# A graph network on one Trainium2 core: drains behind the gathers of GpSimd, and two loaded numbers range-checked

## The chip, the core and the metric

The kernel runs on one core of a Trainium2 chip. It is written by hand: each engine (TensorE or PE, VectorE or DVE, ScalarE or ACT, GpSimd or POOL, SyncE or SP) has its own instruction stream, and the streams meet in semaphores. The metric is the device time of one execution in microseconds (us), as the median of several runs.

## What is computed

6250 nodes with 128 features, 206,250 edges (100,000 random pairs in both directions, and a loop at each node). Three graph convolutions follow each other, then one attention layer with two heads. Cut to what matters:

```python
# three times, on the result of the one before
norm = deg_inv_sqrt[row] * deg_inv_sqrt[col] * edge_weight
xw = einsum('ni,tio->tno', x, W)                     # four edge types
out = segment_sum(xw[edge_type, col] * norm[:, None], row) + b
z = leaky_relu(out, 0.01)
# x = layernorm(x + (x + z1 + z2 + z3) / 4), then the attention
alpha = leaky_relu(a_src[src] + a_dst[dst], 0.2)      # softmax over the edges of a node
out = segment_sum(alpha[:, :, None] * xp[src], dst) + bias
# x = layernorm(x + out)
```

In each layer every edge fetches one row of 128 numbers from a table in HBM and adds it, scaled, to its node.

## The kernel before

**Preparation.** The edges are sorted by node on the chip, and the lists of rows to fetch and of slots are made (`rec_idx`, `gcn_at`, `gat_at`, `gat_need`).

**Layers.** A tile is 128 edges. A layer has 1612 tiles, in 52 turns of 31. For each tile GpSimd issues one indirect DMA (L737, a gather) that fetches 128 rows of 512 bytes into a ring `g_rows` of 93 tiles. `FOURS` cuts a turn into eight groups, seven of four tiles and one of three; the tiles of group u count their landing on semaphore `s_g[u]`. When GpSimd has issued a group it waits until the group before has landed and posts that on `s_land` (`pass_landed`, L711 to L714). Four times in a turn (`SUBS`) it waits, from turn 3 on, for `s_copied`, so that it doesn't overwrite a slot of the ring still to be read (`wait_apart`, L145 to L147: a wait and an increment of a semaphore nobody needs).

ScalarE takes four tiles in a step, 465 steps a layer. It loads their four ring slots and the number of the last tile from `gcn_at` (`slots_of`, L896), waits for `s_gpe` and for `s_land`, and scales the four tiles into `g_step` (L912). TensorE sums them into the nodes by a one-hot matrix `g_hot` that VectorE makes (L1196, L1620), and VectorE adds the sum to `acc` (L1634). In the last 13 or so steps of a layer the table of the next one is made batch by batch (`next_z`, `products`, `rows_of`) and written to HBM; GpSimd starts the next layer when it is there.

**Attention.** 403 groups of four tiles, 451 steps. GpSimd gathers a group into one of eight slots of `a_roll` (L762); from the ninth group on it first loads from `gat_need` which step must be over (L758, range-checked) and waits for it (`sa["cand"]`). Behind its four gathers it waits until the group before has landed and adds one to `s_land`. SyncE goes through the steps: it loads a group number for `e_dst` (L534, range-checked), then group and slot (L540, two numbers in one load, not checked), waits for `s_land`, and copies the slot to `a_rows` (L549). ScalarE, TensorE and VectorE then do the softmax and the sums.

Nothing but these streams sets the order; there is no scheduler.

Of the kernel before, what the change touches and what calls it, by code (L numbers as in the profile page):

```python
# [77 lines left out]
CH = 4  # L78
CCOLS = COLS // CH
# [3 lines left out]
RING = RING_TURNS * TURN  # L83
# [3 lines left out]
GP = 4  # L87
# [6 lines left out]
ROLL = 8  # L94
GAT_GROUPS = EDGES_PAD // (GAT.tiles * P)
AHEAD = BW - 2
SUBS = [(0, 7), (8, 15), (16, 23), (24, TURN - 1)]
FOURS = [range(t, min(t + 4, TURN)) for t in range(0, TURN, 4)]
# [69 lines left out]
def gnn_kernel(nc, x, src, dst, etype, weight, w1, b1, w2, b2, w3, b3, w_gat, att_src, att_dst,  # L168
               bias_gat, out):
    ctx = ExitStack()  # L170
    with ctx:
# [70 lines left out]
        most = sb("most", [BW, 1], F32, sort)  # L242
# [209 lines left out]
        def _(sp):  # L452
# [79 lines left out]
            def body(q):  # L532
                if q.live(2):
                    group = sp.value_load(gat_at[0:1, bass.ds(q.at(2), 1), 0], min_val=0, max_val=GAT_GROUPS - 1)  # L534
                    if q.live(2 - R):
                        wait_apart(sp, sa["cand"], q.at(2 - R, 1, 1), s_apart)
                    sp.dma_start(e_dst[:, q.slot(2), :].unsqueeze(1), dst_groups[:, bass.ds(group, 1), :]
                                 ).then_inc(s_el[q.slot(2)], 16)
                if q.live(0):
                    _, (tile, slot) = nc.values_load_multi_w_load_instructions(  # L540
                        gat_at[0:1, bass.ds(q.at(0), 1), :].rearrange("p g k -> p (g k)"),
                        engines=(mybir.EngineType.SP,), min_val=0, max_val=GAT_GROUPS - 1,
                        skip_runtime_bounds_check_because="a step less the begun blocks, at most the last group")
                    slot = nc.s_assert_within(slot, 0, ROLL - 1,
                                              skip_runtime_bounds_check_because="a group modulo the ring")
                    if q.live(-R):
                        wait_apart(sp, sa["msg"], q.at(-R, 1, 1), s_apart)
                    wait_apart(sp, s_land, tile + (3 * CH * CCOLS + 1), s_apart)
                    sp.dma_start(a_rows[:, q.slot(0), :, :].rearrange("p t k -> p (t k)").unsqueeze(1),  # L549
                                 a_roll[:, bass.ds(slot, 1), :, :].rearrange("p g t k -> p g (t k)")  # L550
                                 ).then_inc(s_ag[q.slot(0)], 16)
# [13 lines left out]
        def _(pool):  # L565
# [150 lines left out]
            for layer in range(3):  # L716
                for k in range(4):
                    pool.wait_ge(s_tw[k], 16 * (layer + 1) * len(range(k, NB, 4)))
                if layer:
                    pool.wait_ge(s_copied, layer * GRP.steps)  # L720
                for q in range(SORT.steps):
                    c, u = divmod(q, CSPANS)
                    if q == 0 and not layer:
                        pool.wait_ge(s_idx0, 1)
                    if (q == 1 or c and u == 0) and not layer:
                        pool.wait_ge(s_idx, c + 1)
                    for low, high in SUBS:
                        steps = CSTEPS * c + u * TURN + high + 1 - RING + AHEAD
                        if u < RING_TURNS:
                            last = u * TURN + high - RING == -1  # L730
                            steps = CSTEPS * c if last else steps - CSTEPS + CCOLS
                        if q >= RING_TURNS:
                            wait_apart(pool, s_copied, layer * GRP.steps - (-steps // GP), s_apart)
                        for t in range(low, high + 1):
                            tile = TURN * q + t
                            at = rec_idx[:, tile:tile + 1] if q else first_idx[:, t:t + 1]
                            pool.indirect_dma_start(  # L737
                                out=g_rows[:, tile % RING, :], out_offset=None, in_=gcn_tables[layer % 2],
                                in_offset=bass.IndirectOffsetOnAxis(ap=at, axis=0),
                            ).then_inc(s_g[t // 4], 16)  # L740
                            n = q * len(FOURS) + t // 4
                            if t == FOURS[t // 4][-1] and n:
                                pass_landed(layer, n - 1)
                pass_landed(layer, SORT.steps * len(FOURS) - 1)
# [11 lines left out]
            for g in range(GAT_GROUPS):  # L756
                if g >= ROLL:
                    need = pool.value_load(gat_need[0:1, g - ROLL:g - ROLL + 1], min_val=1, max_val=GAT.steps)  # L758
                    wait_apart(pool, sa["cand"], need, s_apart)
                for t in range(T):  # L760
                    n = g * T + t
                    pool.indirect_dma_start(  # L762
                        out=a_roll[:, g % ROLL, t, :], out_offset=None, in_=gat_table,
                        in_offset=bass.IndirectOffsetOnAxis(ap=src_plane[:, n:n + 1].bitcast(U32), axis=0),
                    ).then_inc(s_g[g % ROLL], 16)
                if g:
                    wait_apart(pool, s_g[(g - 1) % ROLL], rolled(g - 1), s_land)
            wait_apart(pool, s_g[(GAT_GROUPS - 1) % ROLL], rolled(GAT_GROUPS - 1), s_land)
# [4 lines left out]
        def _(act):  # L773
# [86 lines left out]
            def scale_rows(layer):  # L860
# [32 lines left out]
                        last.then_inc(s_added, 1)  # L893

                def slots_of(q):
                    _, values = nc.values_load_multi_w_load_instructions(  # L896
                        gcn_at[32:33, bass.ds(q.at(0), 1), :].rearrange("p g k -> p (g k)"),
                        engines=(mybir.EngineType.Activation,), min_val=0, max_val=CH * CCOLS - 1,
                        skip_runtime_bounds_check_because="a step less the begun blocks, at most the last tile")
                    return values  # L900

                def scale(q, values):
                    j = q.slot(0) % 3
                    *found, tile = values
                    slots = [nc.s_assert_within(v, 0, RING - 1,
                                                skip_runtime_bounds_check_because="a tile modulo the ring")
                             for v in found]
                    if q.live(-3) or layer:
                        act.wait_ge(s_gpe, q.at(-3, 1, GRP.steps * layer + 1))
                    act.wait_ge(s_land, tile + (CH * CCOLS * layer + 1))  # L910
                    for k in range(GP):
                        last = nc.scalar.activation(g_step[:, j, k, :].unsqueeze(1),  # L912
                                                    g_rows[:, bass.ds(slots[k], 1), :],
                                                    ACT.Copy, scale=rec_w[:, bass.ds(q.at(0, GP, k), 1)])
                    last.then_inc(s_copied, 1)
# [963 lines left out]
```

## Time and profile before

| | us |
|---|---|
| median of 3 runs without a profile | 8958.33 (8957.9 to 8960.3) |
| span of the profiled execution | 11925.3 |
| first gather of the layers starts | 691.5 |
| first gather of the attention starts | 8505.5 |
| last gather starts | 11826.8 |
| GpSimd busy | 6395.8 |

The profiled execution is a third longer than the runs without a profile. Durations of single instructions are taken from it, and waits only where they can be shown to stand in the other runs as well. In the rows, POOL is GpSimd's engine and POOLq its sequencer, which reads the stream, waits for semaphores, loads registers and hands instructions to the engine. "idle before" is time of the engine, and what follows the arrow is who ended it; "issue" means that nothing in the profile did.

### The profile page before, as it was taken

What the parts mean: (1) busy time and instruction counts of PE and PEld (TensorE: products, weight loads), DVE (VectorE), ACT (ScalarE), POOL (GpSimd) and SP (SyncE); (2) the same over time, 40 slices, a digit from 0 to 9 for tenths busy, and PEclk for the clock granted to TensorE, in tenths of its full rate; (3) what the DMA queues carried; (4) which work ended last, traced back from release to release, by engine and by line L of the source; (5) the groups of instructions that cost most, each with busy time, mean ns of one, the idle gap of its engine ahead of it and who ended that gap; (6) DMA issues with size and microseconds to landing.
All of it is one profiled execution on the core that took longest, in us unless ns stands there. A gap on an engine that the chain in (4) does not pass through costs nothing.

```text
span 11925.3 us, 149378 instructions
## 1 busy us (share of the span) xinstructions
PE 5307.0 (45%) x32765; PEld 4105.0 (34%) x32766; DVE 4574.2 (38%) x12940; ACT 3992.0 (33%) x12236; POOL 6395.8 (54%) x6521
## 2 busy tenths in 40 slices
PE   5843434434533434343433434343444444444444
PEld 4632322223322323232322323232344444444444
DVE  9952222222322212222322222222555555555556
ACT  6522222222322222222322222222455454445455
POOL 1656566565456565656466565656344444444443
PEclk9975655656655655565655556555566666666666
DMA  1011111111221111111211111111122222222222
GB/s 47 35 42 43 41 44 43 41 44 41 65 55 44 40 44 40 44 40 44 76 42 44 40 44 40 44 40 44 49 69 70 68 71 69 69 68 69 70 69 65
DMA packets 432687, 612.42 MB, mean 51 GB/s; under 512 B 232038, under 2 KB 249491, under 8 KB 432539
## 3 DMA queue, kind: packets, MB, share of 16 engines
q0 software_dynamic: 208832, 428.96, 13.7%
q1 hardware_dynamic: 223707, 182.02, 4.6%
q14 instruction: 121, 0.99, 0.0%
q8 instruction: 27, 0.44, 0.0%
HBM read 437.29 MB, written 51.28 MB: 41 GB/s over the span
## 4 chain that ended last, share of the span: by engine, by line
another core or an unknown queue 48%; DVE 16%; issue 15%; PE 8%; ACTq 5%; DVEq 4%; ACT 3%; POOL 0%; DMA 0%; POOLq 0%; SPq 0%
DVEq L1604 3%; PE bank L1196 3%; ACT g_step L912 3%; ACTq L896 2%; DVE a_miss L1717 2%; PE wide L1196 2%; DVE g_hot L1620 2%; ACTq L912 1%; DVE acc L1634 1%; DVE a_max L1722 1%; DVE lo_hot L1262 1%; DVE acc L1788 1%; PE bank L1191 1%; DVE v_hot L1387 1%
## 5 line engine op out<-in xcount | busy, mean ns | idle before, releaser
L737 POOL DMA_INDIRECT g_rows<-gcn_table,rec_idx x4743 | 4487.1, 946 | 2894.2 <-ACT g_step L912 1484.6
L912 ACT ACTIVATE g_step<-g_rows,rec_w 128x128 f32 x5580 | 1791.5, 390 | 5679.7 <-remote 4618.4
L762 POOL DMA_INDIRECT a_roll<-gat_table,src_plane x1612 | 1524.6, 946 | 1801.0 <-ACT a_cand L937 1375.4
L1634 DVE TENSOR_TENSOR acc<-acc,bank 128x512 f32 x930 | 637.9, 686 | 3828.8 <-remote 3238.9
L1191 PE MATMUL bank<-zeros 1*128 1x512 bf16 x930 | 490.9, 528 | 2909.9 <-DVE acc L1634 2104.6
L1196 PE MATMUL bank<-g_step,g_hot 128*128 128x128 f32 x7440 | 1621.7, 386 | 128.4 <-issue 50.6
L1196 PEld LDWEIGHTS bank<-g_step,g_hot 128*128 128x128 f32 x7440 | 1391.8, 280 | 487.9 <-issue 487.9
L1222 PE MATMUL bank<-a_msg,a_hot 128*128 128x130 f32 x3608 | 798.9, 389 | 1648.7 <-DVE a_msg L1768 1635.0
L1222 PEld LDWEIGHTS bank<-a_msg,a_hot 128*128 128x128 f32 x3608 | 685.6, 283 | 1786.3 <-DVE a_msg L1768 1452.3
L1191 PEld LDWEIGHTS bank<-zeros 1*128 1x128 bf16 x930 | 89.9, 97 | 3099.0 <-DVE acc L1634 2163.3
L937 ACT ACTIVATE a_cand<-a_miss,a_rows 128x128 f32<-128x128 bf16 x3608 | 1095.9, 386 | 14.9 <-DMA a_rows<-a_roll 8.8
L1634 DVE TENSOR_TENSOR acc<-acc,wide 128x512 f32 x465 | 318.2, 684 | 1879.5 <-remote 1618.0
L1620 DVE TENSOR_TENSOR g_hot<-bank,rec_lo 128x512 f32<-128x512 f32 x1395 | 952.0, 683 | 1.8 <-DVE mv L1677 0.2
L1191 PE MATMUL wide<-zeros 1*128 1x512 bf16 x465 | 244.0, 525 | 1429.6 <-DVE acc L1634 1141.6
L1196 PE MATMUL wide<-g_step,g_hot 128*128 128x128 f32 x3720 | 803.5, 383 | 42.3 <-issue 19.3
L930 ACT ACTIVATE a_hot<-a_miss 128x512 f32<-128x512 bf16 x451 | 284.0, 630 | 1558.0 <-DVE a_miss L1717 1428.6
L1196 PEld LDWEIGHTS wide<-g_step,g_hot 128*128 128x128 f32 x3720 | 690.1, 278 | 220.7 <-issue 220.7
L1213 PE MATMUL wide<-ident,a_cand 128*128 128x128 f32 x3608 | 696.5, 357 | 99.1 <-ACT a_cand L937 83.2
L1213 PEld LDWEIGHTS wide<-ident,a_cand 128*128 128x128 f32 x3608 | 563.9, 186 | 114.5 <-ACT a_cand L937 78.2
L1722 DVE TENSOR_REDUCE a_max<-wide 128x2 f32<-128x1024 f32 x451 | 550.0, 1220 | 107.6 <-remote 69.4
L1741 DVE TENSOR_TENSOR a_z<-bank,a_rows 128x8 f32<-128x8 f32 x451 | 74.0, 164 | 1305.9 <-remote 1302.7
L1191 PEld LDWEIGHTS wide<-zeros 1*128 1x128 bf16 x465 | 44.9, 96 | 1525.1 <-DVE acc L1634 1173.7
(272 smaller groups left out, 5880.3 us busy)
## 6 DMA issues: line engine op xcount, KB each, us to landing
a_rows<-a_roll SPq DMA_DIRECT2D x451, 264.0 KB
g_rows<-gcn_table,rec_idx POOLq DMA_INDIRECT x4743
gcn_table<-rows SPq DMA_DIRECT2D x147, 256.0 KB
a_roll<-gat_table,src_plane POOLq DMA_INDIRECT x1612
e_dst<-by_dst_dst SPq DMA_DIRECT2D x451, 2.0 KB
gat_table<-acc SPq DMA_DIRECT2D x7, 462.0 KB
out_x<-xs SPq DMA_DIRECT2D x6, 448.0 KB
gcn_slots<-nothing SPq DMA_DIRECT2D x4, 468.0 KB, 6.8
```

The lines of the kernel that those rows point to most:

```text
L737: pool.indirect_dma_start(out=g_rows[:, tile % RING, :], out_offset=None, in_=gcn_tables[layer % 2], in_offset=bass.IndirectOffsetOnAxis(a ...
L762: pool.indirect_dma_start(out=a_roll[:, g % ROLL, t, :], out_offset=None, in_=gat_table, in_offset=bass.IndirectOffsetOnAxis(ap=src_plane[ ...
L912: last = nc.scalar.activation(g_step[:, j, k, :].unsqueeze(1), g_rows[:, bass.ds(slots[k], 1), :], ACT.Copy, scale=rec_w[:, bass.ds(q.at(0 ...
L937: last = nc.scalar.activation(a_cand[:, w, h, t, :], a_miss[:, j, t, :], ACT.Identity, scale=-BIG, bias=a_rows[:, j, t, ROW - HEADS + h:RO ...
L1191: nc.tensor.matmul(sums_of(j)[:, :], zeros[0:1, 0:1].to_broadcast([1, P]), zeros[0:1, 0:1].to_broadcast([1, GP * D]), start=True, stop=False)
L1196: last = nc.tensor.matmul(sums_of(j)[:, bass.ds(places[k], D)], g_hot[:, j % 3, k, :], g_step[:, j % 3, k, :], start=False, stop=(k == GP ...
L1213: last = nc.tensor.transpose(wide[:, w, h, t, :], a_cand[:, w, h, t, :], ident[:, :])
L1222: last = nc.tensor.matmul(pv_ps(j), a_hot[:, j, t, :], a_msg[:, j, t, :], start=(t == 0), stop=(t == T - 1))
L1604: _, values = nc.values_load_multi_w_load_instructions(ap, engines=(mybir.EngineType.DVE,), min_val=0, max_val=NB - 1, skip_runtime_bounds ...
L1620: V.tensor_tensor(g_hot[:, j, :, :], spread(iota_ps.unsqueeze(1), [P, GP, P]), spread(lo.unsqueeze(2), [P, GP, P]), ALU.is_equal).then_inc ...
L1634: V.tensor_tensor(dst_ap, dst_ap, sums_of(j).rearrange("p (k d) -> p k d", k=GP), ALU.add).then_inc(s_gadd, 1)
L1722: V.tensor_reduce(a_max[:, m, :], wide[:, m % 2, :, :, :].rearrange("p h t e -> p h (t e)"), AX.X, ALU.max).then_inc(sa["max"], 1)
```

## The change

`pool.drain()` is put behind the last gather of each group: behind the fourth (or third) in a layer, ahead of the wait in `pass_landed`, and behind the fourth in the attention. That is 8 x 52 x 3 = 1248 drains in the layers and 403 in the attention. A drain holds GpSimd's sequencer until its engine is idle.

Two numbers are checked against their range when they are loaded: the last tile's number that ScalarE waits with in a layer's step, and SyncE's group number in an attention step. For that the one load of several numbers is split in two, and the slot in SyncE's load is checked as well.

```diff
@@ SyncE, a step of the attention
-                    _, (tile, slot) = nc.values_load_multi_w_load_instructions(
-                        gat_at[0:1, bass.ds(q.at(0), 1), :].rearrange("p g k -> p (g k)"),
-                        engines=(mybir.EngineType.SP,), min_val=0, max_val=GAT_GROUPS - 1,
...
+                    tile = sp.value_load(gat_at[0:1, bass.ds(q.at(0), 1), 0], min_val=0, max_val=GAT_GROUPS - 1)
+                    slot = sp.value_load(gat_at[0:1, bass.ds(q.at(0), 1), 1], min_val=0, max_val=ROLL - 1)
@@ GpSimd, the layers
                             ).then_inc(s_g[t // 4], 16)
+                            if t == FOURS[t // 4][-1]:
+                                pool.drain()
                             n = q * len(FOURS) + t // 4
                             if t == FOURS[t // 4][-1] and n:
                                 pass_landed(layer, n - 1)
@@ GpSimd, the attention
                     ).then_inc(s_g[g % ROLL], 16)
+                    if t == T - 1:
+                        pool.drain()
                 if g:
                     wait_apart(pool, s_g[(g - 1) % ROLL], rolled(g - 1), s_land)
@@ ScalarE, a step of a layer
                 def slots_of(q):
+                    tile = act.value_load(gcn_at[32:33, bass.ds(q.at(0), 1), GP], min_val=0,
+                                          max_val=CH * CCOLS - 1)
                     _, values = nc.values_load_multi_w_load_instructions(
-                        gcn_at[32:33, bass.ds(q.at(0), 1), :].rearrange("p g k -> p (g k)"),
-                        engines=(mybir.EngineType.Activation,), min_val=0, max_val=CH * CCOLS - 1,
...
+                        gcn_at[32:33, bass.ds(q.at(0), 1), 0:GP].rearrange("p g k -> p (g k)"),
+                        engines=(mybir.EngineType.Activation,), min_val=0, max_val=RING - 1,
...
-                    return values
+                    return *values, tile
```

On ScalarE a layer's step starts with these instructions before (TENSOR_LOAD is a load into registers, REGISTER_ALU and ISA are register arithmetic, and ACTIVATE scales one tile):

```order
L896 TENSOR_LOAD gcn_at
L910 REGISTER_ALU
L912 ISA
L912 ACTIVATE g_step<-g_rows,rec_w 128x128
L912 ISA
```

and with these now:

```order
L896 TENSOR_LOAD gcn_at
L896 ISA x2
L898 TENSOR_LOAD gcn_at
L909 REGISTER_ALU
L911 ISA
L911 ACTIVATE g_step<-g_rows,rec_w 128x128
```

A second load, register arithmetic and a check stand ahead of the first ACTIVATE. On SyncE an attention step, from the second copy of `e_dst` on, is before:

```order
L537 DMA e_dst<-by_dst_dst 128x4
L540 TENSOR_LOAD gat_at
L146 REGISTER_ALU
L549 ISA
L549 DMA a_rows<-a_roll 128x528
```

and now:

```order
L537 DMA e_dst<-by_dst_dst 128x4
L540 TENSOR_LOAD gat_at
L540 ISA x2
L541 TENSOR_LOAD gat_at
L541 ISA x2
L146 REGISTER_ALU
L545 ISA
L545 DMA a_rows<-a_roll 128x528
```

One load has become two with a check behind each, ahead of the copy to `a_rows`. GpSimd's gathers keep their order; the drains stand between them and are not listed in such a view.

## Rows read from the trace of the kernel before

**Rows 1.** Page, part 1: busy us (share of span) x instructions by engine

```profile
PE 5307.0 (45%) x32765; PEld 4105.0 (34%) x32766; DVE 4574.2 (38%) x12940; ACT 3992.0 (33%) x12236; POOL 6395.8 (54%) x6521
```

**Rows 2.** Waits of GpSimd: who <- for whom: us in total, times, longest

```profile
POOL g_rows L737 <- ACT g_step L912: 1484.6, 191, 43.8
POOL a_roll L762 <- ACT a_cand L937: 1375.4, 312, 11.6
```

**Rows 3.** Groups by line on GpSimd: xcount | busy us, mean ns | idle before

```profile
L737 POOL DMA_INDIRECT g_rows<-gcn_table,rec_idx x4743 | 4487.1, 946 | 2894.2 <-ACT g_step L912 1484.6 <-issue 1246.4 <-DMA g_rows<-gcn_table,rec_idx 162.8
L762 POOL DMA_INDIRECT a_roll<-gat_table,src_plane x1612 | 1524.6, 946 | 1801.0 <-ACT a_cand L937 1375.4 <-issue 410.2 <-DMA a_roll<-gat_table,src_plane 11.9
...
L737 POOL DMA_INDIRECT g_rows<-gcn_table,first_idx x93 | 90.3, 971 | 225.0 <-DMA gcn_table<-rows 185.6 <-issue 24.7 <-DVE first_idx L1506 12.0
...
L748 POOL MEMSET acc<- 128x14 f32 x7 | 0.9, 124 | 125.1 <-ACT acc L858 125.1
```

**Rows 4.** Timeline of GpSimd, three stretches: start us, us, what, [idle before <-releaser]

```profile
691.47 1.00 POOL L737 DMA_INDIRECT g_rows<-gcn_table,first_idx  x1 [11.97 <-DVE first_idx L1506]
...
2121.42 0.95 POOL L737 DMA_INDIRECT g_rows<-gcn_table,rec_idx  x1 [0.30 <-DMA g_rows<-gcn_table,rec_idx]
...
2128.93 0.94 POOL L737 DMA_INDIRECT g_rows<-gcn_table,rec_idx  x1 [0.30 <-issue]
...
11826.75 0.95 POOL L762 DMA_INDIRECT a_roll<-gat_table,src_plane  x1 [0.30 <-issue]
```

**Rows 5.** Timeline of ScalarE in a layer, a step that waits for nobody

```profile
2113.31 1.28 ACT L912 ACTIVATE g_step<-g_rows,rec_w 128x128 f32 x4 [0.63 <-issue]
```

**Rows 6.** Timeline of VectorE in the attention, the same line in two steps

```profile
9004.72 0.17 DVE L1741 TENSOR_TENSOR a_z<-bank,a_rows 128x8 f32<-128x8 f32 x1 [7.43 <-remote]
...
9008.89 0.17 DVE L1741 TENSOR_TENSOR a_z<-bank,a_rows 128x8 f32<-128x8 f32 x1
```

**Rows 7.** Timeline of GpSimd around waits, in a layer and in the attention

```profile
1621.09 0.94 POOL L737 DMA_INDIRECT g_rows<-gcn_table,rec_idx  x1 [6.22 <-ACT g_step L912]
...
8660.60 0.94 POOL L762 DMA_INDIRECT a_roll<-gat_table,src_plane  x1 [6.21 <-ACT a_cand L937]
...
8666.85 0.95 POOL L762 DMA_INDIRECT a_roll<-gat_table,src_plane  x1 [0.31 <-issue]
```

**Rows 8.** Line 147 on GpSimd's sequencer, three single instructions: duration ns, first to last start

```profile
L147 POOLq EVENT_SEMAPHORE  x1: 17/17/17, 1620.3 to 1620.3; - x1
...
L147 POOLq EVENT_SEMAPHORE  x1: 17/17/17, 8659.8 to 8659.8; - x1
...
L147 POOLq EVENT_SEMAPHORE  x1: 17/17/17, 8666.9 to 8666.9; - x1
```

**Rows 9.** Line 758 between 8666 and 8668 us: duration ns, first to last start

```profile
L758 POOLq TENSOR_LOAD <-gat_need x1: 293/293/293, 8667.0 to 8667.0; - x1
...
L758 POOLq SEQ_ASSERT  x1: 18/18/18, 8667.5 to 8667.5; - x1
```

**Rows 10.** Timeline of GpSimd at the start of the program

```profile
0.39 0.12 POOL L1868 MEMSET const-uint8-127<- 128x1 uint8 x1
0.91 0.24 POOL L566 IOTA iota<- 128x128 f32 x1 [0.40 <-POOLq L1868]
```

**Rows 11.** Line 1868 on GpSimd's sequencer: xcount: duration ns, first to last start

```profile
L1868 POOLq EVENT_SEMAPHORE  x2: 17/17/17, 0.6 to 0.7; - x2
...
L1868 POOLq DRAIN  x1: 189/189/189, 0.4 to 0.4; - x1
```

**Rows 12.** Stretches: PE, PEld, DVE, ACT, POOL busy us (x), PEclk, DMA share, GB/s

```profile
1659.50:1660.00 0.50, 0.00 (x0) 0.00 (x0) 0.00 (x0) 0.00 (x0) 0.05 (x1) 0.50 0.00 0
1660.00:1660.50 0.50, 0.00 (x0) 0.00 (x0) 0.00 (x0) 0.00 (x0) 0.00 (x0) 0.50 0.43 123
```

**Rows 13.** Timeline of TensorE and of ScalarE in a layer, one step

```profile
1606.52 2.07 PE L1196 MATMUL bank<-g_step,g_hot 128*128 128x128 f32 x8 [0.26 <-issue]
...
1619.03 1.28 ACT L912 ACTIVATE g_step<-g_rows,rec_w 128x128 f32 x4 [12.75 <-remote]
```

More of the change, by code:

```diff
@@ L539, in body @@
                 if q.live(0):
-                    _, (tile, slot) = nc.values_load_multi_w_load_instructions(
-                        gat_at[0:1, bass.ds(q.at(0), 1), :].rearrange("p g k -> p (g k)"),
-                        engines=(mybir.EngineType.SP,), min_val=0, max_val=GAT_GROUPS - 1,
-                        skip_runtime_bounds_check_because="a step less the begun blocks, at most the last group")
-                    slot = nc.s_assert_within(slot, 0, ROLL - 1,
-                                              skip_runtime_bounds_check_because="a group modulo the ring")
+                    tile = sp.value_load(gat_at[0:1, bass.ds(q.at(0), 1), 0], min_val=0, max_val=GAT_GROUPS - 1)
+                    slot = sp.value_load(gat_at[0:1, bass.ds(q.at(0), 1), 1], min_val=0, max_val=ROLL - 1)
                     if q.live(-R):
@@ L895, in slots_of @@
                 def slots_of(q):
+                    tile = act.value_load(gcn_at[32:33, bass.ds(q.at(0), 1), GP], min_val=0,
+                                          max_val=CH * CCOLS - 1)
                     _, values = nc.values_load_multi_w_load_instructions(
-                        gcn_at[32:33, bass.ds(q.at(0), 1), :].rearrange("p g k -> p (g k)"),
-                        engines=(mybir.EngineType.Activation,), min_val=0, max_val=CH * CCOLS - 1,
-                        skip_runtime_bounds_check_because="a step less the begun blocks, at most the last tile")
-                    return values
+                        gcn_at[32:33, bass.ds(q.at(0), 1), 0:GP].rearrange("p g k -> p (g k)"),
+                        engines=(mybir.EngineType.Activation,), min_val=0, max_val=RING - 1,
+                        skip_runtime_bounds_check_because="a tile modulo the ring")
+                    return *values, tile
                 def scale(q, values):
                     j = q.slot(0) % 3
[L904 to L907, printed above, removed]
+                    *slots, tile = values
                     if q.live(-3) or layer:
```

## The prediction

> **What bounds the kernel now.** I read the page's head and engine totals first [rows 1]. GpSimd (POOL) is busy 54% of the span, more than any other engine, and no engine is near full. The waits of POOL come next [rows 2]: 1484.6 us (191 times) for ScalarE's copies in the layers and 1375.4 us (312 times) for ScalarE in the attention. The profiled execution took 11925 us, the median without a profile is 8958, so it must first be settled which of these waits exist in the timed runs.
>
> Count GpSimd's work. There are 4743 + 93 gathers in the three layers and 1612 in the attention, 6448 in all, 946 ns each [rows 3]. In a stretch without waits one starts every 1.25 us (2121.42 to 2128.93 is 6 intervals of 1.252), with 0.30 us "issue" between them [rows 4]. 6448 x 1.252 = 8073 us. Around them stand parts with no gather: 691 us until the first, two layer changes of 93 us (185.6), 125 us ahead of the attention and 98 us behind the last gather [rows 3, 4]: 1100 us. Together 9173 us. The same from the other side: the profiled span without the waits for ScalarE, 11925 - 1485 - 1375 + 503 x 0.30 (the normal gap that each of these 503 waits contains) = 9216. The median of 8958 is below both. So in a timed run GpSimd issues gathers without a pause from the first to the last, the waits for ScalarE belong to the profiled execution, and the missing 215 us are a preparation or a pitch a little shorter than under the profile (1.22 us would do). The other engines have room beside it: where ScalarE isn't waiting, a layer step of four tiles takes it 1.28 + 0.63 = 1.91 us [rows 5] against GpSimd's 5.0; a VectorE step of the attention takes 4.17 us [rows 6], 451 x 4.17 = 1881 us against GpSimd's 1612 x 1.25 = 2018.
>
> **The drains.** A drain stops GpSimd's sequencer until the engine is idle; only then does it read the landing semaphore, post s_land and send the next gather. Now it works ahead. At 8666.9 it posts the landing of one group [rows 8] while the second gather of the next group is just starting [rows 7]; that group's two last gathers are already queued, and the load of the following number (0.29 us), its range check [rows 9] and the wait for ScalarE all vanish behind them: the gaps stay 0.30. A drain gives up exactly this overlap. There are 8 in each of 52 turns of 3 layers, 1248, and 403 in the attention, 1651 in all.
>
> Price of one in a layer. The trace has two cases in which GpSimd's queue was empty: in the layers the waiting instruction runs at 1620.3 and the gather starts at 1621.09; in the attention 8659.8 and 8660.60 [rows 7, 8]. I take 0.75 us and 0.77 us from wait to start. The one DRAIN of GpSimd in the trace starts at 0.37 (0.4 in its row), lasts 189 ns, and ends 0.05 us behind the last MEMSET's end (0.39 + 0.12); the next semaphore instruction is at 0.6 [rows 10, 11]: about 0.1 us from idle to the first wait. So 0.1 + 0.75 = 0.85 us stand between two gathers where 0.30 do now: +0.55. 1248 x 0.55 = 686 us. In front of every second group of turns 3 to 51 stands a second wait, for s_copied, at about 0.1 us (the step from the wait at 8666.9 to the load at 8667.0 [rows 8, 9]): 588 x 0.1 = 59 us.
>
> Price of one in the attention. Behind the drain come the landing wait, then the load at +0.1 us, the range check until +0.6 (8666.9 to 8667.5 [rows 8, 9]), the wait for ScalarE at about +0.65 and 0.77 to the start: 0.1 + 0.65 + 0.77 = 1.5 against 0.30, +1.2. 395 groups have the load: 474 us; the first eight 0.55 each: 4.
>
> None of this lies beside other work, since GpSimd is the bound. Drains: 686 + 59 + 478 = 1223 us.
>
> The bounds of this price. Below: the engine's shortest restart from an empty queue is the IOTA that starts at 0.91 behind the semaphore instruction at 0.7 [rows 10, 11], 0.2 us; 0.1 + 0.2 is the gap that is there now, so a gather that restarts as fast as an IOTA costs nothing. I stay with the gathers' own rows. Above: the 0.30 us between two gathers may be work of the engine behind the recorded end. Then the drain ends up to 0.30 later: + 1651 x 0.30 = 495, in all 1718 us. The Trainium skill (Perfetto Trace Analysis, DMA Instruction — SWDGE) says for this engine that the recorded end is the last descriptor written and that the instruction finishes after it; by that page the price lies between my value and this upper end.
>
> **What is queued behind a drain.** On GpSimd: the post of s_land for the group before (now at the second gather of a group, then behind its fourth, 2.5 us later) and all later gathers. Who waits for the post is ScalarE in the layers, SyncE in the attention. GpSimd may run at least 45 tiles or 8 groups ahead, some 50 us, so the late post delays only the ends of stages, by 2.5 us each; I leave it out.
>
> **The range checks.** GpSimd's own load with its check takes 0.5 us of its sequencer (8667.0 to 8667.5 [rows 9]); I take 0.6 us for one on SyncE or ScalarE too, where a load may first have to wait for the instructions before it. SyncE gets a second load and two checks in each of 451 attention steps, about 0.8 us, 361 us if it were bare. It lies beside GpSimd's 6.2 us per group: nothing. ScalarE gets a second load and a check in each of 1395 steps: a step goes from 1.91 to 2.5 us, beside GpSimd's 5.0 or more for the same four tiles: hidden, except where no gather is left. There, at a layer's end, ScalarE still has about 28 steps (some 15 of catching up, then the last 13 among the next layer's rows): 28 x 0.6 = 17 us a layer, 50 in all; part of it lies beside VectorE's and TensorE's work, so I take 35 out of 0 to 50. If GpSimd were not the bound, all 1395 would be bare: 837 us.
>
> **The sum.** 8958 + 1223 + 35 = 10216 us. The durations are of the profiled execution; the base is the median, since the profile's own excess (2967 us) is waits that the drains would partly fill there.
>
> **The rivals.**
> Slower, as forecast (queue lost at each drain): 10216, between 9700 and 10850. For it: every number above is this engine's own. Against: the restart was seen only behind waits, never behind a drain.
> Cheap drain: the sequencer's work on the next gather is mostly hidden and only 0.1 to 0.2 us is lost per drain, 165 to 330 us: 9120 to 9320 with the rest. The IOTA's short restart [rows 10, 11] speaks for it; that 403 of these gathers sit behind a load and a check speaks against.
> Drain waits for the data: after a gather that ended at 1659.55, packets still move at 1660.0 to 1660.5 [rows 12], so a drain that lasts until they have landed takes 1.0 us more: + 1651 = 11870. The one DRAIN in the trace [rows 11] had no DMA behind it and can't tell.
> No loss, or a gain: if GpSimd waits for ScalarE in the timed runs too, a drain only fills such a wait. The trace shows how: ScalarE's step at 1619.03 starts after 12.75 us of waiting, 10 us after TensorE's last matmul of the step before has ended (1606.52 + 2.07) [rows 13], in one of GpSimd's pauses (6.22 us ahead of 1621.09 [rows 7]). If gathers hold other engines' releases back, pauses let them through sooner. It decides once these waits exceed 1223 us in a timed run, and gives 8958 or less, say 8850. The count above leaves no room for them.
> The drain does nothing (the engine is idle when it comes): 8958 + 35. The steady 0.30 us gap [rows 4] with a queue behind it speaks against.
>
> **How the numbers follow.** Queue lost 0.73; cheap 0.11; waits for data 0.07; filled waits or a gain 0.04; nothing 0.03; the rest, some other stall, 0.02. The likeliest gives 10215. The range runs from 9250 (half of the cheap case) to 10850 (the upper end of the price with the range checks' 50 and some more), which leaves about 0.17 outside. A measurement of this kernel can tell about 0.2% from no change. Faster by more: 0.03 (a gain). Within: 0.03. Slower: 0.94.
>
> **What the changed profile would show.** Three gaps of 0.30 us between gathers and every fourth 0.85 in the layers, 1.5 in the attention; DRAIN of 2 to 3 us each on GpSimd, since it is reached while gathers are queued; s_land's post behind the fourth gather. Wrong would be: every fourth gap still near 0.30 or 0.45 (cheap), or near 1.9 and 2.5 (waits for data); other engines' busy times unchanged in all cases. If the gaps are as said and the time moved by less than half of 1223, the claim that GpSimd bounds the timed runs falls.

## The result, and the profile after

| | before | after |
|---|---|---|
| median without a profile | 8958.15 us | 13031.51 us |
| lowest to highest, 4 runs each | 8957.9 to 8960.3 | 13030.99 to 13036.31 |
| span of the profiled execution | 11925.3 | 13034.2 |

The change makes the kernel slower by 45%: the ratio is 1.4548, with a 95% interval of 1.4527 to 1.4569. That is 4073 us for 1651 drains, 2.47 us each. The forecast was 10215 us, 1257 us more than before. Its direction was right and the measured cost was 3.2 times the forecast one.

Read this profile with one caution. The profiled execution of before took a third longer than its other runs, that of after took the time of its other runs. A comparison of the two profiles would show 1109 us, not 4073. So the profile of the first experiment, in which the drains alone are missing (span 8945.1, as long as its other runs), is what after has to be compared with.

The engines of after (page, part 1: busy us, share of the span, instructions), which answer to [rows 1], and the shares of the chain that ended last:

```profile
PE 5925.3 (45%) x32765; PEld 4641.6 (36%) x32766; DVE 4687.3 (36%) x12940; ACT 3955.9 (30%) x12236; POOL 6397.1 (49%) x6521
...
issue 44%; POOL 34%; POOLq 15%; DVE 3%; PE 2%; ACT 1%; DMA 1%; ACTq 0%; DVEq 0%; SPq 0%
```

GpSimd is busy as long as before, 6397 us against 6396. None of its work takes longer; the time lies between its instructions. Half of the chain is GpSimd (POOL and its sequencer POOLq), and most of the rest is "issue", idle time that nothing in the profile explains. The 15% of POOLq are mostly the records of the drains where they lie beside a gather that is still running. Behind the last gather of a group a drain leaves no busy time of the engine and no semaphore event, so there the profile shows its cost as "issue".

GpSimd's groups of after by line (busy us, mean ns, idle time ahead and who ended it), which answer to [rows 3]:

```profile
L733 POOL DMA_INDIRECT g_rows<-gcn_table,rec_idx x4743 | 4491.3, 947 | 4285.3 <-issue 4269.4 <-ACT g_step L911 15.9
L760 POOL DMA_INDIRECT a_roll<-gat_table,src_plane x1612 | 1524.6, 946 | 1693.2 <-issue 1571.4 <-ACT a_cand L936 118.1 <-DMA gat_table<-acc 3.7
...
L733 POOL DMA_INDIRECT g_rows<-gcn_table,first_idx x93 | 91.4, 983 | 157.8 <-issue 84.3 <-DMA gcn_table<-rows 62.6 <-DVE first_idx L1505 10.8
```

A gather still takes 947 ns. Ahead of the layers' gathers GpSimd sits idle for 4285 us and hardly any of it is a wait for ScalarE. The timeline of GpSimd in a layer and in the attention (start us, us, what, idle before) shows where:

```profile
3001.52 0.95 POOL L733 DMA_INDIRECT g_rows<-gcn_table,rec_idx  x1 [2.66 <-issue]
...
3005.28 0.95 POOL L733 DMA_INDIRECT g_rows<-gcn_table,rec_idx  x1 [0.30 <-issue]
3008.75 0.95 POOL L733 DMA_INDIRECT g_rows<-gcn_table,rec_idx  x1 [2.52 <-issue]
...
11009.41 0.95 POOL L760 DMA_INDIRECT a_roll<-gat_table,src_plane  x1 [3.30 <-issue]
```

Three gaps of 0.30 us are as before [rows 4]; every fourth is 2.5 to 2.7 us in this stretch of a layer and 3.30 in the attention. Of the two in the lines, the longer one (2.66) has the second wait, for `s_copied`, in it. The prediction had 0.85 and 1.5 for these.

What happens in the gap of 2.52 us is seen from three answers of the trace: the drain of this group on GpSimd's sequencer (xcount: duration ns min/median/max, first and last start), the pieces of the chain in order of time (L710 is the first instruction that has a record behind the drain, it posts `s_land`), and the stretches of half a microsecond (engines' busy us, PEclk, DMA share, GB/s).

```profile
L738 POOLq DRAIN  x1: 5287/5287/5287, 3002.7 to 3002.7; - x1
```

```profile
3006.22 1.77 issue
3007.99 0.02 POOLq L710
3008.01 0.74 issue
```

```profile
3006.00:3006.50 0.50, 0.00 (x0) 0.00 (x0) 0.00 (x0) 0.00 (x0) 0.22 (x1) 0.50 0.01 0
3006.50:3007.00 0.50, 0.00 (x0) 0.00 (x0) 0.00 (x0) 0.00 (x0) 0.00 (x0) 0.50 0.17 57
3007.00:3007.50 0.50, 0.00 (x0) 0.00 (x0) 0.00 (x0) 0.00 (x0) 0.00 (x0) 0.50 0.25 74
3007.50:3008.00 0.50, 0.00 (x0) 0.00 (x0) 0.00 (x0) 0.00 (x0) 0.00 (x0) 0.50 0.00 0
```

The sequencer reaches the drain at 3002.7, with the second gather of the group just starting. The fourth gather ends on the engine at 3006.22. The drain holds for another 1.77 us, until 3007.99, and in this time the rows of that gather arrive: the DMA share is 0.01, then 0.17 and 0.25, then 0. Then 0.76 us pass until the next gather starts, the restart that the prediction took from [rows 7, 8]. So a gap of 2.52 is 1.77 of drain and 0.75 of restart.

Everyone else waits for GpSimd. The first entry of the waits of after (who, for whom: us, times, longest):

```profile
ACT g_step L911 <- POOLq L710: 6860.5, 1204, 20.3
```

ScalarE waits 1204 times for the post of line 710. In the profile of before it was GpSimd that waited for ScalarE [rows 2]. That isn't the work of the drains: in the profile of experiment 1, without a drain, ScalarE already waits 1096 times for this post, 3784 us in all.

### The profile page after: what moved, and what is told of

Read it like the earlier page. It is cut to its first block, busy times and chain, and to the rows that moved or that the text cites. A ratio compares the mean times of both kernels' runs of the same rounds, so it can differ in the third digit from the quotient of the medians.

```text
span 13034.2 us, 159230 instructions
## 1 busy us (share of the span) xinstructions
PE 5925.3 (45%) x32765; PEld 4641.6 (36%) x32766; DVE 4687.3 (36%) x12940; ACT 3955.9 (30%) x12236; POOL 6397.1 (49%) x6521
## 4 chain that ended last, share of the span: by engine, by line
issue 44%; POOL 34%; POOLq 15%; DVE 3%; PE 2%; ACT 1%; DMA 1%; ACTq 0%; DVEq 0%; SPq 0%
POOL g_rows L733 26%; POOLq L738 10%; POOL a_roll L760 8%; POOLq L765 3%; POOLq L756 1%; ACT a_cand L936 1%; DVE lo_hot L1261 1%; DVE v_hot L1386 1%; PE wide L1081 0%; DMA a_rows<-a_roll 0%; DVE p_hot L1261 0%; DVE hi_hot L1261 0%; PE wide L1159 0%; PE wide L1095 0%; POOLq L147 0%
## 5 line engine op out<-in xcount | busy, mean ns | idle before, releaser
L733 POOL DMA_INDIRECT g_rows<-gcn_table,rec_idx x4743 | 4491.3, 947 | 4285.3 <-issue 4269.4
L1195 PE MATMUL bank<-g_step,g_hot 128*128 128x128 f32 x7440 | 1884.3, 433 | 3399.5 <-ACT g_step L911 3391.8
L1195 PEld LDWEIGHTS bank<-g_step,g_hot 128*128 128x128 f32 x7440 | 1620.5, 321 | 3845.6 <-issue 3845.6
L760 POOL DMA_INDIRECT a_roll<-gat_table,src_plane x1612 | 1524.6, 946 | 1693.2 <-issue 1571.4
L1195 PE MATMUL wide<-g_step,g_hot 128*128 128x128 f32 x3720 | 946.2, 435 | 1798.5 <-ACT g_step L911 1798.5
L1195 PEld LDWEIGHTS wide<-g_step,g_hot 128*128 128x128 f32 x3720 | 814.1, 323 | 2021.6 <-issue 2021.6
L1212 PE MATMUL wide<-ident,a_cand 128*128 128x128 f32 x3608 | 821.9, 403 | 1497.1 <-ACT a_cand L936 1497.0
L1212 PEld LDWEIGHTS wide<-ident,a_cand 128*128 128x128 f32 x3608 | 656.4, 210 | 1532.7 <-ACT a_cand L936 1278.4
L1221 PEld LDWEIGHTS bank<-a_msg,a_hot 128*128 128x128 f32 x3608 | 753.3, 307 | 94.5 <-DVE a_msg L1767 73.6
L1767 DVE SCALAR_TENSOR_TENSOR a_msg<-bank,a_rows 128x520 f32<-128x520 f32 x451 | 315.1, 699 | 1031.2 <-ACT bank L948 1031.2
L591 POOL DMA_INDIRECT gcn_slots<-run,at_u x52 | 285.5, 5491 | 390.8 <-issue 380.8
L1716 DVE TENSOR_TENSOR a_miss<-bank,a_lo 128x256 bf16<-128x256 f32 x902 | 375.0, 416 | 0.1
```

The costliest lines, as they stand in the source:

```text
L733: pool.indirect_dma_start(out=g_rows[:, tile % RING, :], out_offset=None, in_=gcn_tables[layer % 2], in_offset=bass.IndirectOffsetOnAxis(a ...
L760: pool.indirect_dma_start(out=a_roll[:, g % ROLL, t, :], out_offset=None, in_=gat_table, in_offset=bass.IndirectOffsetOnAxis(ap=src_plane[ ...
L1195: last = nc.tensor.matmul(sums_of(j)[:, bass.ds(places[k], D)], g_hot[:, j % 3, k, :], g_step[:, j % 3, k, :], start=False, stop=(k == GP ...
L1212: last = nc.tensor.transpose(wide[:, w, h, t, :], a_cand[:, w, h, t, :], ident[:, :])
L1221: last = nc.tensor.matmul(pv_ps(j), a_hot[:, j, t, :], a_msg[:, j, t, :], start=(t == 0), stop=(t == T - 1))
```

## The experiments

Two theories were compared at the start. **Landing**: a drain of GpSimd holds until all that GpSimd has asked of the DMA engines has landed. **Engine idle**, the prediction's own: it holds until the engine has done its work, and something else (a fixed toll of the drain, or the late post of `s_land`) makes the rest. All kernels of the network start from the kernel after, with both range checks in, so the drains alone without these checks weren't tried.

**1. The range checks alone.**

```diff
-                            if t == FOURS[t // 4][-1]:
-                                pool.drain()
...
-                    if t == T - 1:
-                        pool.drain()
```

> The changed kernel without any drain: the two range checks alone. Theory (all of the loss is in the drains): 8958 us, at most 35 more at the layers' ends. Rival (the split loads on ScalarE or SyncE reach the path): 9300 or more, up to 837 us more if ScalarE's steps were bare. The profiled execution should again be near 11900, if its excess over the timed runs belongs to a stream of gathers without drains.

Measured: 8949.75 us (10 runs, 8946.94 to 8951.04) beside 8948.27 of before, ratio 1.0001 (0.9991 to 1.0011). The checks cost nothing that the runs can tell. They are there: the number of ScalarE's first loads and of the range checks behind them (SEQ_ASSERT), with the duration of one (ns), and then GpSimd's waits in this trace, are

```profile
L892 ACTq TENSOR_LOAD <-gcn_at x1395: 268/273/974, 745.8 to 6834.1; - x200
L892 ACTq SEQ_ASSERT  x1395: 18/18/29, 746.5 to 6834.6; - x200
```

```profile
POOL g_rows L733 <- issue: 1371.9, 4503, 0.3
POOL a_roll L758 <- issue: 478.8, 1571, 0.3
...
POOL a_roll L758 <- ACT a_cand L932: 5.2, 17, 0.3
```

This profile is the picture of the kernel without drains that the prediction had to infer. GpSimd waits 4503 and 1571 times, never longer than 0.3 us: a gather follows a gather from end to end, and the long waits for ScalarE of [rows 2] aren't there. The expectation that this profile would again be near 11900 us did not come true: its span is 8945.1. The idle time by group gives the account of the change:

```profile
L733 POOL DMA_INDIRECT g_rows<-gcn_table,rec_idx x4743 | 4490.1, 947 | 1445.0 <-issue 1346.0 <-DMA g_rows<-gcn_table,rec_idx 96.6 <-ACT g_step L907 2.4
L758 POOL DMA_INDIRECT a_roll<-gat_table,src_plane x1612 | 1522.8, 945 | 494.5 <-issue 478.8 <-DMA a_roll<-gat_table,src_plane 7.0 <-ACT a_cand L932 5.2
...
L733 POOL DMA_INDIRECT g_rows<-gcn_table,first_idx x93 | 90.2, 969 | 94.7 <-DMA gcn_table<-rows 55.3 <-issue 25.9 <-DVE first_idx L1501 11.9
```

With drains the idle time ahead of these three groups is longer by 2840 (4285.3 - 1445.0), 1199 (1693.2 - 494.5) and 63 us (157.8 - 94.7), 4102 in all. The spans differ by 4089 (13034.2 - 8945.1). So the whole loss is idle time of GpSimd ahead of a gather; the other engines and the ends of stages add nothing that shows.

**2 and 3. The drains of one part alone.** Kernel 2 leaves out the second of the two removed pieces above (the drain in the attention), kernel 3 the first (the drains in the layers).

> Drains in the three layers alone (1248). Theory landing (a drain lasts until the gathers' data has landed, gaps of 2.53 to 2.65 us as in the changed kernel's trace, 2.3 more than the normal 0.30): 8958 + 1248 x 2.3 = 11830 us. Theory of the forecast (only the queue is lost, 0.55 each): 9700. If the losses of layers and attention do not add up (this plus the one with attention drains alone is not 8958 + 4073), they share a limit.

> Drains in the attention alone (403). Theory landing (gaps of 3.28 us, 2.97 more): 8958 + 403 x 2.97 = 10155 us. Theory of the forecast (1.2 each): 9440. If the sum with the layers' kernel falls short of 4073, part of the loss is shared.

Measured: the layers' 1248 drains alone give 11827.87 us, ratio 1.3218 (1.3196 to 1.3240), +2880 beside 8948.27. The attention's 403 alone give 10149.3, ratio 1.1342 (1.1323 to 1.1361), +1201. The two add up to 4081 against 4073 for both, so the two parts share no limit. One costs 2.31 us in a layer and 2.98 in the attention, which is the gaps of the timeline less the 0.30 that was there. The difference of 0.67 fits what stands behind the drain in the attention, the load and check of `gat_need`; the prediction had 0.65 for it (1.2 - 0.55), or 0.59 between its averages, in which the waits for `s_copied` are spread over the layers' drains (478 / 403 - 745 / 1248).

**4. Every second drain.**

```diff
-                            if t == FOURS[t // 4][-1]:
+                            if t == FOURS[t // 4][-1] and t // 4 % 2:
...
-                    if t == T - 1:
+                    if t == T - 1 and g % 2:
```

> Drains behind every second group alone (624 in the layers, each ahead of two waits, and 201 in the attention). Theory landing, each drain for itself: 624 x 2.35 + 201 x 2.97 = 2063, so 11020 us. Rival (what costs is that gathers get behind once and for all, or a fixed toll of draining at all): clearly not half of 4073.

Measured: 11135.31 us, ratio 1.2442 (1.2421 to 1.2463), +2187, which is 150 more than half of 4073, and 124 more than expected. GpSimd's timeline behind such a drain shows a longer gap, 2.88 us instead of 2.66 or 2.52:

```profile
3011.99 0.94 POOL L733 DMA_INDIRECT g_rows<-gcn_table,rec_idx  x1 [2.88 <-issue]
```

So a drain isn't independent of what lies before it: with eight gathers since the last drain instead of four, one costs about 0.2 us more. This was not expected by either theory and led to experiments 9 and 10.

**5. No drain, but a wait for the group's own landing.** GpSimd waits for the landing semaphore of the group that it has just issued, not of the one before.

```diff
-                            if t == FOURS[t // 4][-1]:
-                                pool.drain()
                             n = q * len(FOURS) + t // 4
-                            if t == FOURS[t // 4][-1] and n:
-                                pass_landed(layer, n - 1)
-                pass_landed(layer, SORT.steps * len(FOURS) - 1)
+                            if t == FOURS[t // 4][-1]:
+                                pass_landed(layer, n)
...
-                    if t == T - 1:
-                        pool.drain()
-                if g:
-                    wait_apart(pool, s_g[(g - 1) % ROLL], rolled(g - 1), s_land)
-            wait_apart(pool, s_g[(GAT_GROUPS - 1) % ROLL], rolled(GAT_GROUPS - 1), s_land)
+                wait_apart(pool, s_g[g % ROLL], rolled(g), s_land)
```

> No drain; GpSimd waits behind each group for the landing of that same group instead of the one before. Theory landing (the drain is in effect this wait): the gap is the landing 1.57 us after the gather's end, about 0.05 to see it, and the restart 0.75 (attention: load, check and 0.77), so 2.07 to 2.17 more than 0.30 in the layers and 2.73 in the attention: 8958 + 2640 + 1100 = 12700 us. Rival (a drain costs by itself, whatever has landed): the landing lies beside other work, and this kernel stays below 11500.

Measured: 12772.62 us, ratio 1.4260 (1.4236 to 1.4284), beside 8957.31: 94% of what the drains cost (3815 of 4073 us), without one drain. Its timeline:

```profile
3001.18 0.94 POOL L733 DMA_INDIRECT g_rows<-gcn_table,rec_idx  x1 [2.31 <-DMA g_rows<-gcn_table,rec_idx]
```

Here the profile names the releaser, the DMA of the gather. From the gather's end to its landing it is 2.31 - 0.75 of restart, about 1.56 us. The chain of this trace gives it directly (start us, us; the DMA piece counts from the start of the gather, which keeps the engine for 0.94 us):

```profile
2997.93 2.47 DMA g_rows<-gcn_table,rec_idx
...
3000.43 0.02 POOLq L710
```

2.47 - 0.94 is 1.53 us to the landing, and 0.02 later comes the post. A drain's 1.77 is this landing and 0.2 us more. Here `s_land` is posted for the group itself and as soon as it has landed, and still 94% of the cost is there; so the late post of `s_land` isn't what costs.

**6. The wait of 5 and a drain behind it.** When the drain comes, everything has landed.

```diff
                             if t == FOURS[t // 4][-1]:
                                 pass_landed(layer, n)
+                                pool.drain()
...
                 wait_apart(pool, s_g[g % ROLL], rolled(g), s_land)
+                pool.drain()
```

> As the kernel that waits for its own group, and then a drain, when nothing of GpSimd's is under way. Theory landing: a drain with all landed costs 0.05 to 0.2 us: 80 to 330 us more than without, about 12900. Rival (a drain behind DMAs takes a fixed 1.7 us from the engine's end on, or from its own start on): 1651 x 1.7 = 2800 more, about 15500.

Measured: 13315.66 us, ratio 1.4867 (1.4842 to 1.4891), +543 over kernel 5 or 0.33 us a drain, more than the 80 to 330 us that were expected. A second landing or a fixed toll of 1.7 us a drain would have given 15500. The drain's own record has shrunk from 5.3 us, in which the rest of the group and the landing lay, to

```profile
L740 POOLq DRAIN  x1248: 282/364/4649, 700.1 to 9920.5; - x179
```

So it is mainly the landing that the drain of the kernel after waits for. But 364 ns with nothing left to wait for is twice the 189 ns of [rows 11].

**7. Engine idle, made by hand.** No drain; a MEMSET of one column behind each group, and a wait for its semaphore. The engine has then finished its gathers; their data may be on the way.

```diff
+            def engine_idle():
+                idles[0] += 1
+                nc.gpsimd.memset(idle[:, :], 0.0).then_inc(s_idle, 1)
+                pool.wait_ge(s_idle, idles[0])
...
-                                pool.drain()
+                                engine_idle()
...
-                        pool.drain()
+                        engine_idle()
```

> No drain; behind each group a memset of one column on GpSimd and a wait for its semaphore: this waits until the engine has done its gathers, but not for their data. It is what the forecast took a drain for. By the forecast's prices (queue lost: memset about 0.1, 0.1 to see it, restart 0.75 or in the attention 1.4, less 0.30): 0.65 in a layer, 1.3 in the attention: 8958 + 811 + 524 = 10290 us, between 9900 and 10700. Theory landing says the same, and that the difference to the changed kernel is the wait for the data. Rival (the memset itself waits for the data): near 13000.

Measured: 10412.39 us, ratio 1.1623 (1.1604 to 1.1643). This is the event that the prediction priced, and it lies 2% above the forecast of 10215, inside its range. The gaps in a layer and in the attention:

```profile
3005.96 0.94 POOL L742 DMA_INDIRECT g_rows<-gcn_table,rec_idx  x1 [0.30 <-issue]
3006.90 0.12 POOL L711 MEMSET idle<- 128x1 f32 x1
3007.93 0.95 POOL L742 DMA_INDIRECT g_rows<-gcn_table,rec_idx  x1 [0.91 <-POOL idle L711]
```

```profile
9006.10 0.12 POOL L711 MEMSET idle<- 128x1 f32 x1
9007.69 0.95 POOL L769 DMA_INDIRECT a_roll<-gat_table,src_plane  x1 [1.47 <-issue]
```

From gather to gather 1.03 us in this place of a layer (0.12 + 0.91) and 1.59 in the attention, of which 0.12 is the MEMSET. Without the MEMSETs themselves (1651 x 0.12 = 198 us) the 1455 us of this kernel are 1257. The MEMSET also starts right at the gather's end: the 0.30 us between two gathers is not work of the engine that the MEMSET has to wait for. The upper end of the prediction's price (0.30 more per drain) had stood on that.

**8. GpSimd alone, the drain behind different things.** One small kernel without the network: 12 times each a gather of 128 rows of 128 bytes, of 512 bytes and of 5120 bytes with a drain behind it, four gathers of 512 bytes and a drain, a gather, its landing and a drain, a plain DMA and a drain, a MEMSET and a drain, and this again while SyncE's own DMA of 3 MB is under way.

```python
for r in range(12):
    gather(one[:, r, :], x, s_b)
    pool.drain()
...
for r in range(12):
    gather(landed[:, r, :], x, s_e)
    pool.wait_ge(s_e, 16 * (r + 1))
    pool.drain()
```

> Not the network: GpSimd alone, 12 times each a gather of 128 rows of 128, 512 and 5120 bytes and a drain; four gathers of 512 bytes and a drain; a gather, a wait for its landing and a drain; a plain DMA of GpSimd and a drain; a memset and a drain; and the same while SyncE's load of 3.1 MB is under way. Theory landing: the drain ends 0.2 us after the last landing, so its end moves with the size of the row (1.7 us after the gather's end at 512 bytes, clearly more at 5120), it is short behind the wait (0.2 us) and behind the memsets, SyncE's load or not. Rival (fixed): 1.7 us after the gather's end at all sizes, and also behind the wait. Rival (the drain waits for every DMA of the core): some 10 us behind the first memset under SyncE's load.

Measured: the drains, in the order just given (128, 512, 5120 bytes, four gathers, landed, plain DMA, MEMSET, MEMSET beside SyncE's DMA), by duration:

```profile
L59 POOLq DRAIN  x12: 2471/2526/2790, 13.6 to 47.2; - x12
...
L63 POOLq DRAIN  x12: 2796/2852/2941, 50.2 to 87.2; - x12
...
L67 POOLq DRAIN  x12: 4647/5074/5179, 90.6 to 151.8; - x12
...
L72 POOLq DRAIN  x12: 5332/5356/5388, 158.8 to 239.0; - x12
...
L77 POOLq DRAIN  x12: 113/113/126, 247.7 to 285.4; - x12
...
L80 POOLq DRAIN  x12: 2087/2148/2361, 286.0 to 315.3; - x12
...
L84 POOLq DRAIN  x12: 157/158/177, 317.5 to 320.2; - x12
...
L89 POOLq DRAIN  x12: 152/157/166, 321.4 to 323.8; - x12
```

The timeline for the three row sizes, and the times from issue to landing (part 6, last number, us):

```profile
17.14 0.97 POOL L53 DMA_INDIRECT small<-in_x,idx  x1 [2.14 <-issue]
...
53.89 0.95 POOL L53 DMA_INDIRECT one<-in_x,idx  x1 [2.48 <-issue]
...
96.34 0.94 POOL L53 DMA_INDIRECT large<-in_x,idx  x1 [4.62 <-issue]
```

```profile
direct<-in_x POOLq DMA_DIRECT2D x12, 64.0 KB, 2.1
small<-in_x,idx POOLq DMA_INDIRECT x12, 2.2
one<-in_x,idx POOLq DMA_INDIRECT x12, 2.6
large<-in_x,idx POOLq DMA_INDIRECT x12, 4.8
...
load<-in_x SPq DMA_DIRECT2D x1, 0.5 KB, 13.3
```

The page gives 0.5 KB for SyncE's load; the kernel loads 48 x 128 rows of 512 bytes with it, 3.1 MB. The last of the eight kinds of drain runs from 321.4 to 323.8, and this load moves its data in that time (stretch: POOL busy us, PEclk, DMA share, GB/s):

```profile
323.00:324.00 1.00, 0.41 (x5) 1.00 0.96 311
```

This settles what a drain waits for. The engine's work on a gather is 0.95 us whatever the size of the rows. The gap behind it grows with the time to landing: landing at 2.2, 2.6 and 4.8 us, that is 1.25, 1.65 and 3.85 us after the engine's end, and gaps of 2.14, 2.48 and 4.62, each 0.77 to 0.89 us longer. A drain behind a plain DMA of GpSimd lasts 2.15 us where the DMA takes 2.1. A drain behind a MEMSET lasts 0.16 us, and as short while SyncE's DMA needs 13.3 us: this transfer of another engine doesn't matter.

**9. A drain once a turn.** One behind the last group of a turn (156 in all) and one behind every eighth group of the attention (50).

```diff
-                            if t == FOURS[t // 4][-1]:
+                            if t == FOURS[t // 4][-1] and t // 4 == 7:
...
-                    if t == T - 1:
+                    if t == T - 1 and g % 8 == 7:
```

> One drain behind each turn of 31 tiles in the layers (156) and behind every eighth group in the attention (50). From the earlier traces a drain ends 0.07 us after the last landing with 1 gather since the last drain, 0.20 with 4 and 0.36 with 8: about 0.04 per gather. Theory tail (this goes on): 1.4 us with 31 or 32 gathers, gaps of 3.8 and 4.4 us, 156 x 3.5 + 50 x 4.1 = 751 more, 9705 us. Theory landing alone, tail at most 0.36 us: gaps of 2.8 and 3.4, 545 more, 9500. A toll in proportion to the number of drains, 4073 x 206 / 1651 = 508: 9460. The traces' gaps decide between them.

Measured: 9674.91 us beside 8943.97, ratio 1.0817 (1.0799 to 1.0835), +731 for 206 drains or 3.55 each. The landing alone would have given 9500, the landing with a part that grows with the gathers 9705. The gaps in a layer and in the attention:

```profile
3001.28 0.94 POOL L733 DMA_INDIRECT g_rows<-gcn_table,rec_idx  x1 [3.61 <-issue]
...
8009.43 0.94 POOL L760 DMA_INDIRECT a_roll<-gat_table,src_plane  x1 [4.40 <-issue]
```

3.61 less 0.75 of restart and 1.56 of landing leaves 1.3 us behind 31 gathers, against 0.2 behind 4.

**10. The length of a drain with everything landed.** The small kernel again: 1, 2, 4, 8 or 16 gathers, a wait for their landing, a drain; six times each.

> Not the network: 6 times each 1, 2, 4, 8 and 16 gathers of 512 bytes, a wait for their landing, and a drain, so that the drain's own length is left. Theory tail (about 0.04 us per gather since the last drain): 0.11 us with one (as seen), some 0.15, 0.25 to 0.36, 0.4 to 0.55 and 0.75 to 0.9 with 2, 4, 8 and 16. Rival (the 0.36 us in the network come from its other traffic): 0.11 at all counts.

Measured, in that order:

```profile
L48 POOLq DRAIN  x6: 113/113/143, 16.6 to 33.7; - x6
...
L53 POOLq DRAIN  x6: 198/198/201, 38.3 to 62.1; - x6
...
L58 POOLq DRAIN  x6: 364/364/371, 69.3 to 106.7; - x6
...
L63 POOLq DRAIN  x6: 691/691/691, 119.1 to 182.7; - x6
...
L68 POOLq DRAIN  x6: 1344/1344/1344, 205.4 to 322.1; - x6
```

About 0.03 us and 0.082 us for each gather since the last drain (113 to 198 for one more, 691 to 1344 for eight more). The growth was expected, at half this rate (0.75 to 0.9 us with 16). Four give 364 ns, exactly what kernel 6 showed. Where the drain is reached while the gathers still land, as in the kernel after, about half of this is hidden: 0.2 us instead of 0.36 with four gathers, 1.3 with 31.

## Why the prediction was wrong, step by step

**What bounds the kernel: right.** The claim that the timed runs never wait for ScalarE came from counting 6448 gathers at their pitch. Experiment 1 shows it in a profile: no wait of GpSimd ahead of a gather of the lists exceeds 0.3 us. The "missing 215 us" of that count were not a shorter preparation or pitch, as it guessed (in experiment 1 the first gather starts at 691.58, and the pitch is 1.25), but the ends of the layers and the start of the attention: ahead of the tables and the MEMSETs GpSimd waits 55.3 and 53.3 us in experiment 1 where [rows 3] have 185.6 and 125.1, 202 us less.

**The number of drains and their being bare: right.** 1651 drains, all on GpSimd's path, none beside other work. The idle time ahead of GpSimd's gathers grew by 4102 us, the span by 4089.

**The restart and the lost overlap: right.** 0.75 us from the end of the wait to the gather's start stands again in after (3007.99 to 3008.75), and the attention's extra was 0.67 against 0.65 or 0.59. Experiment 7 made the event that was priced and cost 1455 us (10412.39 - 8957.31), or 1257 without its MEMSETs, against the priced 1223.

**"A drain stops GpSimd's sequencer until the engine is idle": this step failed.** From it came the first term, 0.1 us from the end of the last gather to the end of the drain. Measured it is 1.77: about 1.56 for the rows to land and 0.2 that grow with the gathers. The missing 1.67 us x 1651 are 2757 us; with the 1223 this is 3980 of the 4073. The 93 us left, 0.06 a drain, aren't put down to anything. The Trainium skill (PSUM — Partial Sum Buffer, Engine vs sequencer instructions) says that a drain "waits for the engine to go fully idle". Experiments 5 to 8 show that for GpSimd this includes its DMAs, which a reader of the engine's busy time doesn't see.

**How the step came about.** The only drain in the trace stood behind a MEMSET [rows 11]; experiment 8 repeats that case with 0.16 us. The prediction itself said that this row can't tell, named the right mechanism as a rival, and still gave it 0.07 and left it out of the range. For 73% it had only the reading of a word and a row that did not bear on the question. With two mechanisms open and 1650 us between them, the range should have reached to 11870 at least. Its own chances also leave more outside the range than the 0.17 it states: 0.07 + 0.04 + 0.03 + 0.02 and half of the 0.11 make 0.21.

**The price of that rival was too small as well.** It took 1.0 us, from packets that moved 0.5 to 1.0 us after the gather's end [rows 12]. The end of movement isn't the landing: in the stretches of after the data stop by 3007.5 and the drain ends at 3007.99. With 1.67 instead of 1.0 the rival would have given 8958 + 1223 + 2757 + 35 = 12973, within 0.5% of the result.

**The range checks: hidden, as said, and more so.** The prediction took 35 us at the ends of layers; experiment 1 shows 1.5 us in 8948 with an interval of 9 us either way, so at most some 10 us of it can be there. The cover was named rightly (GpSimd's 5.0 us for four tiles).

**What the changed profile would show.** The three gaps of 0.30 us were right, and nearly so were the unchanged busy times of GpSimd, ScalarE and VectorE (at most 2.5% from [rows 1]). TensorE's was not unchanged: 5307 us before, 5656 in experiment 1 and 5925 in after, where the granted clock was 0.573 instead of 0.624 (means of the executions); TensorE isn't what the chain waits for, and this costs nothing that shows. The gaps of 0.85 and 1.5 were wrong, and for the case that drains wait for the data the text had 1.9 and 2.5, where 2.5 and 3.3 stand. The drains' records were forecast at 2 to 3 us and are 5.3, since the sequencer is held with nearly three gathers and the landing still to come.

**What stays open.** Why the profiled execution of before took 11925 us, with waits for ScalarE of a size that no other profile of this study shows, isn't explained. Kernel 1, which differs from it by the range checks alone, was profiled without these waits, so it isn't the lack of drains, and the mean granted clock was no lower (0.634 against 0.624 in kernel 1). There is only this one profile of it. Nor was it tried what the 0.082 us per gather are spent on.

## What to carry to other kernels

A drain on GpSimd behind DMAs that GpSimd has issued is a wait for their landing, and a restart of an empty engine behind it; where order is wanted, a semaphore wait that lags by a group cost nothing here (gaps of 0.30 us in experiment 1): the next group's gathers had been issued when it was reached. If a drain is needed, few of them are much cheaper: one in eight groups cost 8% here, one in each 45%. And when an operation's cost hangs on what it waits for, look for a row in which that thing was still outstanding; if there is none, the range has to hold both readings.

## What the runs showed of the hardware

The length of a drain on GpSimd grows with its own DMAs that have yet to land: 2.5, 2.9 and 5.1 us behind a gather of 128 rows of 128, 512 and 5120 bytes. It also depends on how many gathers GpSimd has issued since the last one, even when all have landed: 113, 198, 364, 691 and 1344 ns for 1, 2, 4, 8 and 16. SyncE's load didn't make it longer (157 ns with it and 158 without). A gather of 128 rows keeps GpSimd for 0.95 us, with rows of 128 as with rows of 5120 bytes. And a landing semaphore comes later than the last visible movement of data: about 0.3 to 0.5 us here (an estimate: movement until some time between 3007.3 and 3007.5, and a landing 1.56 us after the gather's end at 3006.22, at 3007.8, by the time that experiment 5 measured).
